# Four output pieces half a tile sooner, and the output copy split between ScalarE and GpSimd

## The reference

```python
logits = jnp.einsum('bhid,bhjd->bhij', q, k) * SCALE
logits = jnp.einsum('bhij,gh->bgij', logits, Wpre)
attn = jax.nn.softmax(logits, axis=-1)
attn = jnp.einsum('bhij,gh->bgij', attn, Wpost)
out = jnp.einsum('bhij,bhjd->bhid', attn, v)
out = out.transpose(0, 2, 1, 3).reshape(b, n, DIM)
return out @ Wout.T + bout
...
x = _layernorm(x + _L0_attn_ref(x, ...), axis=-1)
```

## Time and profile before

| what | value |
|---|---|
| median of 3 runs | 8371.17 us (8367.39 to 8371.35) |
| the profiled execution | 8358.64 us, span 8356.8 us |
| granted TensorE clock, mean | 0.984 of full speed |
| TensorE busy | 7996.8 us, 96% |
| VectorE busy | 7605.1 us, 91% |
| ScalarE busy | 6848.0 us, 82% |
| GpSimd busy | 6046.9 us, 72% |

### The profile page before, as it was taken

The page is one execution under the profiler, slowest core; times in us unless marked ns, Lnnn a source line. Parts: engine busy times, 40 slices in busy tenths (PEclk is TensorE's granted clock), DMA queues, the critical chain, the costliest instruction groups (busy, mean ns, idle before and its releaser), DMA issues.

```text
span 8356.8 us, 449859 instructions
## 1 busy us (share of the span) xinstructions
PE 7996.8 (96%) x182764; PEld 4649.9 (56%) x182764; DVE 7605.1 (91%) x13390; ACT 6848.0 (82%) x11648; POOL 6046.9 (72%) x12006
## 2 busy tenths in 40 slices
PE   7999999998899999999889999999979999999997
PEld 4555555555555555555545555555554555555554
DVE  7999999997899999999789999999978999999996
ACT  5888888886688888888568888888857888888884
POOL 6777777774677777777477777777737777777773
PEclk9999999998999999999899999999989999999998
DMA  1011111112101111111211111111121011011112
GB/s 53 23 28 27 26 26 27 26 27 91 34 24 27 27 26 26 27 28 26 89 35 25 26 27 26 27 26 27 26 88 36 25 26 28 25 27 26 27 26 93
DMA packets 265756, 284.04 MB, mean 34 GB/s; under 512 B 41089, under 2 KB 252673, under 8 KB 261377
## 3 DMA queue, kind: packets, MB, share of 16 engines
q1 hardware_dynamic: 263680, 255.07, 11.3%
HBM read 78.75 MB, written 39.85 MB: 14 GB/s over the span
## 4 chain that ended last, share of the span: by engine, by line
PE 73%; DVE 12%; issue 10%; POOL 1%; ACT 1%; DVEq 1%; DMA 0%; SPq 0%; POOLq 0%; ACTq 0%
PE psS L1248 47%; PE psP L1267 15%; PE psO L1282 6%; DVE big L878 5%; DVE pl L906 2%; DVE spare L867 2%; PE psM L1293 1%; ACT big L694 1%; DVE ot L889 1%; PE psS L1378 1%; PE psM L1308 1%; PE psS L1407 1%; PE psS L1209 0%; DVE nb L867 0%; PE psS L1196 0%
## 5 line engine op out<-in xcount | busy, mean ns | idle before, releaser
L1248 PE MATMUL psS<-KH,AX 64*128 64x512 f16 x32768 | 3928.4, 377 | 52.0 <-DMA AX<-AX 50.1
L694 ACT ACTIVATE big<-psP 128x512 f16<-128x512 f32 x4096 | 2222.4, 595 | 826.2 <-PE psP L1267 822.9
L878 DVE SCALAR_TENSOR_TENSOR big<-psP,big 128x512 f16<-128x512 f32 x4096 | 2613.9, 679 | 175.5 <-ACT big L694 174.0
L675 ACT ACTIVATE pr<-psS,nb 128x1024 f32<-128x1024 f32 x2048 | 2289.7, 1118 | 192.9 <-DVE nb L867 190.1
L1248 PEld LDWEIGHTS psS<-KH,AX 64*128 64x128 f16 x32768 | 1451.5, 95 | 1513.5 <-DMA AX<-AX 51.7
L704 ACT ACTIVATE ph<-pr 128x1024 f16<-128x1024 f32 x2048 | 2166.8, 1058 | 32.3
L1248 PE MATMUL psS<-KL,AX 64*128 64x512 f16 x16384 | 2106.3, 377 | 0.0
L906 DVE TENSOR_TENSOR pl<-pr,ph 128x1024 f16<-128x1024 f32 (+1 forms) x2048 | 2078.3, 1015 | 0.0
L1267 PE MATMUL psP<-rh,ph 64*128 64x64 f16 x32768 | 1671.7, 191 | 131.4 <-DVE big L878 112.0
L1267 PEld LDWEIGHTS psP<-rh,ph 64*128 64x128 f16 x32768 | 1468.7, 95 | 557.9 <-DVE big L878 395.9
L1267 PE MATMUL psP<-rl,ph 64*128 64x64 f16 x32768 | 1667.0, 191 | 4.7 <-issue 4.3
(11 more groups left out here) (137 smaller groups left out, 6286.4 us busy)
## 6 DMA issues: line engine op xcount, KB each, us to landing
AX<-AX SPq DMA_DIRECT2D x2048, 64.0 KB, 2.0
ph<-in_xT SPq DMA_DIRECT2D x16, 512.0 KB, 8.7
xr<-in_x SPq DMA_DIRECT2D x64, 128.0 KB, 2.3
Q<-in_w SPq DMA_DIRECT2D x8, 1024.0 KB, 7.2
out<-V SPq DMA_DIRECT2D x16, 512.0 KB, 3.7
d_x<-x SPq DMA_DIRECT2D x60, 128.0 KB, 2.0
d_xn<-xn SPq DMA_DIRECT2D x60, 128.0 KB, 2.0
d_lg<-lg SPq DMA_DIRECT2D x60, 128.0 KB, 2.0
```

What stands on the lines that cost most here:

```text
L675: a.activation(pr[:, p, h * N2:(h + 1) * N2], psS[:, 2 * h:2 * h + 2, :].rearrange("p c n -> p (c n)"), ACT.Exp, bias=nb[:, p, h:h + 1], s ...
L694: a.activation(PT[:, hf * JH:(hf + 1) * JH, :, 0, i0:i0 + HQ], psP[:, ih, :].rearrange("p (j g i) -> p j g i", j=JH, g=H), ACT.Copy, scale ...
L878: v.scalar_tensor_tensor(out=PT[:, js, :, 1, i0:i0 + HQ], in0=psP[:, ih, :].rearrange("p (j g i) -> p j g i", j=JH, g=H), scalar=MDROP, in ...
L1248: mm = pe.matmul(psS[:, 2 * hp + half, :], AX[rows, k8, kq, s_, :], K_[rows, kq, hp, :], start=n == 0, stop=n == len(steps) - 1, tile_posi ...
```

## The change

Two things are changed.

The pieces. Before, in the slots t = 2 and 10, TensorE issues piece 0 inside the first scores block, piece 1 behind it, piece 2 inside the second scores block and piece 3 behind that. Now piece 0 goes one slot earlier, to t = 1 or 9, behind the second scores block; piece 1 is inside the first scores block of slot 2 or 10, piece 2 behind it, piece 3 inside the second.

The copy. Before, VectorE reads psO twice, in slot 3 or 11, behind each pair of mixed_low. Now ScalarE copies all of psO (128x512, float32) to a new SBUF tile oraw, behind the second pair of mixed_high of that slot, and GpSimd adds the two halves of oraw to ot, behind its low. The last group of each batch is still copied by VectorE.

```diff
+        oraw = sb("oraw", [P, GQ * P])
+        s_or = sem("s_or")
...
+                def out_sum(n, half, R):
+
+                    g.wait_ge(s_or, b * (NIT * 2 - 1) + n + 1)
+                    g.wait_ge(s_y, R + 1)
+                    parts = oraw[:, :].rearrange("p (q s i) -> p q s i", q=GQ, s=2)
+                    apart(g)
+                    g.tensor_tensor(ot[:, :, half * GI:(half + 1) * GI],
+                                    parts[:, :, 0, :], parts[:, :, 1, :], ALU.add).then_inc(s_oc, 2)
...
                     if one:
                         low(T - 1, t_1, first and t < 3)
+                    if t % TG == 3 and not (first and t < TG) and it < NIT:
+                        out_sum(it * 2 + t // TG - 1, (t // TG + 1) % 2, b * NIT + it - (1 if t < TG else 0))
                     roots(it, t, 2)
...
+                def out_raw(n):
+
+                    Gd = b * (NIT * 2) + n
+                    a.wait_ge(s_F, (Gd + 1) * NC + NC)
+                    a.wait_ge(s_oc, Gd * 2 + 1)
+                    a.activation(oraw[:, :], psO[:, :], ACT.Copy).then_inc(s_or, 1)
...
                     mixed(2)
                     mixed(3)
+                    if t % TG == 3 and not (first and t < TG) and it < NIT:
+                        out_raw(it * 2 + t // TG - 1)
                     if live:
                         exps(T, t, 1, early)
...
-                    copied(it, t, first, 0)
                     rows(it, t, 1)
...
-                    copied(it, t, first, 1)
                     if live:
                         low(T, t, 0, first and t < 2)
...
-                    def piece(c):
+                    def piece(c, at):
 
-                        if t % TG == 2 and not (first and t < TG):
-                            output(T - 2, (b * NIT + it) * 2 + t // TG - 1, (c,))
+                        if t % TG == at and not (first and t < TG) and it < NIT:
+                            output(T - at, (b * NIT + it) * 2 + t // TG - 1, (c,))
 
                     if live:
-                        scores(T, it, t, 0, first and t < 1, (lambda: piece(0),))
-                    piece(1)
+                        scores(T, it, t, 0, first and t < 1, (lambda: piece(1, 2),))
+                    piece(2, 2)
...
-                        scores(T, it, t, 1, first and t < 1, (lambda: piece(2),))
-                    piece(3)
+                        scores(T, it, t, 1, first and t < 1, (lambda: piece(3, 2),))
+                    piece(0, 1)
```

More of the change, by code:

```diff
@@ L1022, in combine @@
                     v.tensor_scalar(ew[:, :], ew[:, :], er[:, 0:1], None, ALU.mult).then_inc(s_C, 1)
[L1024 to L1028, removed]
                 def rows(it, t, place):
```

## The result

The change made the kernel slower: 8413.81 us (median of 5 runs, 8404.55 to 8424.92) against 8368.42 us for the kernel before on the same chip, a ratio of 1.0054 with a 95% interval of 1.0039 to 1.0068. The 8368.42 is the median of five runs, the first three of which gave the 8371.17 that the forecast started from. The forecast was 8352 us with a range to 8395 us. The profiled execution took 8404.55 us, its span is 8401.4 us against 8356.8 us, and the mean granted clock is 0.984 in both, so these 44.6 us are not the clock's.

A forecast was written before the change was run, and what follows sets the result against it. TensorE bounds the kernel (73% of the chain), its turns waiting for VectorE's mixed_low. Terms of -28, +17 and -7 us, -19 with roundings, took the 8371.17 us median to 8352 us; range 8295 to 8395.

The forecast's parts named there:

- The reading of the lock: VectorE's low and GpSimd's instructions: whoever starts first holds the other off; low of 512 saves 0.52, low of 1024 loses 0.49.
- The add's and the copy's durations: GpSimd's add of the two halves takes 0.72 us; ScalarE's copy of 512 columns from PSUM takes 0.6 us.
- ScalarE is covered: In slot 11 ScalarE's copy hides in 0.47 us of idle time: cost 0, margin about 0.1 us; uncovered 0.6.
- Rival 3: ScalarE's copy isn't covered and delays mixed_high, mixed_low and the turn: 8390 us, or 8426 in all groups; chance 0.20.
- Slot 2: VectorE's idle 0.78 us behind half_max takes up most of the 1.01 lost cover, leaving +0.22 us per group.
- Rivals 1 and 2: Lost cover in slot 10 isn't felt, 8298 us, chance 0.17; VectorE's low has no lock wait, 8321 us, chance 0.10.
- rival 1: Slot 10 takes the lost cover like slot 2; each group gains min(0.69, its stall), 73 us: 8298 us, chance 0.17.
- the sum: Per group: -0.47 us in 60 copied in slot 3, +0.32 in 52 copied in slot 11; 12 others -7 us together.
- the shift of slot 10: Scores end 1.01 us later before an unmoved turn; VectorE has no idle there, so the whole +1.01 goes through.
- the saving of slot 11: VectorE without the two reductions and the 0.52 lock gains 1.18 us per group, less 0.49 for GpSimd's add.
- My sentence on what would show it: The turn's waits for mixed_low: about 0.6 us in a group copied in slot 3, 0.8 in one copied in slot 11.
- The 0.2 that I gave the slower side: Chance of a measurably slower kernel, 0.19, of which only 0.02 came from the forecast and the rest from Rival 3.

The follow-up runs named there:

- copy_late: The kernel before with both of VectorE's reductions behind the second pair of mixed_low, none behind the first: 8313.69 us, 0.9931.
- move_only: The kernel before with only the four pieces moved, VectorE still copying the bank: 8457.56 us, 1.0112.
- split_only: The kernel before with only the copy split between ScalarE and GpSimd, pieces where they were: 8306.71 us, 0.9931.
- half_moved: half_add with the pieces moved as in the change: 8368.68 us, 0.9997 to the kernel before.
- add_short: The changed kernel with GpSimd's add cut from 64 columns of each head group to 1: 8350.87 us, 0.9989 to the kernel before.
- add_apart: split_only with GpSimd's add of the slot-11 groups moved to slot 2 of the next iteration (last iteration: slot 15): 8292.74 us, 0.9912.
- half_add: The kernel before, but ScalarE copies half the bank and VectorE adds the other half from PSUM in one instruction; pieces unmoved: 8273.79 us, 0.9885.
- behind_split: split_only with two pieces behind each scores block and none inside: 8356.47 us, 0.998 to the kernel before.

## Why the prediction was wrong

Which steps held:
- **The reading of the lock** held. Low of 1024 columns: 1.73 behind the add, 0.52 more than 1.21 (forecast 0.49); low of 512: 0.68. copy_late shows the 0.52 by itself.
- **The add's and the copy's durations** held: 0.725 (forecast 0.72) and 0.603 (forecast 0.6).
- **ScalarE is covered** held: without 504 of its 512 columns the ratio is 1.0047 against 1.0054, within the intervals. Rival 3 falls, though the time lies in its half of the scale: mixed_low's waits for mixed_high did grow as it would have them (174.0 to 230.8), but they do so with the moved pieces (226.6 in move_only) and not with the copy (176.4 in split_only).
- **Slot 2** held: of 1.01 a stall of 0.24 was left at slot 3's turns, forecast 0.22.
- **Rivals 1 and 2** fall: the lost cover is felt (move_only), and so is the lock (1.73). But rival 1's way of counting, min(saving, stall) for each group, was nearer: it gives 73 us for the split alone, and split_only brought 0.69%, some 58.

What failed is **the sum**, in its term for the groups copied in slot 11: forecast +0.32 us each, measured 1.55 - 0.56 = +0.99. It had put the shift of slot 10 (+1.01) and the saving of slot 11 (-0.69) on one path and let the turn of slot 12 feel the difference. Three things went another way:
- The shift reaches two turns of slot 11 before VectorE gets to where it saves. TensorE pays there and then: 1.16 us, not 1.01. The excess of 0.15 is one more lock. In 48 of the 52 groups the low of 1024 columns between the two turns (2500.21) takes 1.42 in place of 1.22, and in each of them GpSimd's L488 was already running. In iteration 6 VectorE is first, the low takes 1.22, and the two stalls are 0.75 and 0.24, together 0.99:

```profile
2500.15 1.74 POOL L488 TENSOR_TENSOR at<-Q,wpre_q 128x128 f32<-128x128 f32 x2
...
2986.70 1.22 DVE L928 TENSOR_TENSOR pl<-pr,ph 128x1024 f16<-128x1024 f32 x1
2986.91 1.62 POOL L488 TENSOR_TENSOR at<-Q,wpre_q 128x128 f32<-128x128 f32 x2 [0.23 <-issue]
```

  half_moved and add_short have four such groups each, with 0.99 and 0.98 (move_only has eight, with 1.12); in the kernel before, this low took 1.22 in all 52. So the shift is worth the forecast's 1.01, and it pushes VectorE into a lock as well.
- A saving behind a stall only takes away the stall that stands behind it. That was 0.55, so 0.55 came back, not 0.69. In half_moved the same is larger: one path would leave 0.56 - 0.85 + 1.01 = 0.72 of stalls, measured are 1.22, the shift's own 1.17 and next to nothing else.
- The add makes GpSimd late, and the lock comes again a slot later, as some 0.2 on each of two lows; stalls of 0.36 us per group are the end of it. It isn't in my sum at all; I had followed the add to its own end and one low, not GpSimd's next instructions against VectorE's. In split_only, where these stalls are 0.32, moving the add away removes them (add_apart); in the kernel after, shortening it does (add_short).

0.15 + 0.14 + 0.36 = 0.65, the miss of 0.67 per group.

In the groups copied in slot 3 I had -0.47, measured 0.74 - 1.05 = -0.31. The shift's 0.24 is as forecast, so 0.55 came back where I had taken 0.69 off. The stall at slot 4's first turn, 0.50, is gone, and at its second 0.49 is left of 0.57; with the short add that goes too (0.00), so what is left is the add's. Last, the pieces themselves run with more pauses: starts more than 0.12 us apart within the pieces add up to 35.2 us against 20.9. Together 48 x 0.99 - 52 x 0.31 + 14.3 = 45.7 us, and the spans differ by 44.6. The 24 groups at the batches' edges aren't in this account, so it is good to some us, not better.

The move costs the same whatever stands in slot 11: 1.0112 on the kernel before, 1.0054 / 0.9931 = 1.0124 on split_only, 0.9997 / 0.9885 = 1.0113 on half_add. That is what it has to be if it is paid ahead of the copies. On the kernel before, +1.01 per group would have been about right (move_only: 1.75 - 0.56 = 1.19); the mistake lay in letting the split pay for it.

My sentence on what would show it ("0.8 in one copied in slot 11") looked for one stall in slot 12; the trace has two in slot 11, none in slot 12, and two small ones in slots 13 and 14 (0.16 and 0.19 in the mean). From the first piece of one group to that of the next the mean time grew from 58.51 to 59.50 us over the slot-11 copy and fell from 62.01 to 61.94 over the other: the loss is all of the first kind. The 0.2 that I gave the slower side was on ScalarE, the wrong mechanism; my own +1.01 with nothing set against it, 52 x 1.01 = 53 us, was in the working and should have been a rival.

What stays open: why the moved pieces run with more pauses, and how much of the 0.36 is the add's own lock and how much those of the slot behind. The extra lock in the shift is read from groups that differ within one kernel; no run took it away.

## What to carry to other kernels

Walk the stalls in the order of time: a delay is paid at the first consumer that has no slack, and a saving that comes after it buys back only the stalls that lie behind the saving. Work between a producer's input and the consumer of its output is cover, and moving it away can cost its whole length where the producer has no idle time, as the 1.01 us of a piece did here. When work is handed to an engine that shares a resource with the critical one, follow that engine's next slots too, not only the new instruction; and try a cheaper place for the old instruction first (copy_late) or the smallest new one (half_add).

## What the runs showed of the hardware

- VectorE's low, on two SBUF inputs, is held off by a GpSimd instruction that began first, if only by 0.08 us (2506.88 and 2506.96: 1.73 in place of 1.21) or 0.06 (2500.15 and 2500.21: 1.42), and not by one that began later (2986.70 and 2986.91: 1.22). Making GpSimd late by 0.72 brought its low and VectorE's to overlap in the slot behind, where they had missed each other by 0.05. The hold is some 0.12 us shorter than what is left of GpSimd's record: 0.65 left gave 0.52 (3092.92), 0.64 gave 0.52 (2506.96), 0.38 gave 0.24 (2762.39), 0.31 gave 0.19 (2758.67). The Trainium skill (SBUF — State Buffer, section Who interferes with whom) has the contention, and these rows agree with it; the repetition in later slots is only in these runs.
- VectorE's add of 256 columns with one input in PSUM takes 0.413 us in the mean of 124, as long as one strided reduction of 256 columns (0.41), and the low of 1024 columns behind it stays at 1.21 (at 2497.04 in half_moved).
- TensorE can pause inside a run of short matmuls with nothing in the profile that it waits for. In behind_split the 128 matmuls of two pieces (1.90 us) and the 48 of a turn stand in a row, and starts more than 0.12 us apart inside turns come to 99.0 us (86 of them), against 19.1 us (53) in split_only, where 12 matmuls of a scores block stand between the two pieces. All but 5 of the 86 are in slots 2 and 10, in the turns behind the pieces. I had not expected it, and no run shows the cause.
